# Four filler matmuls taken out of the head stage of an mLSTM block, and one group of transposes issued one step earlier

## What is computed

```
q, k, v, o_pre = projections of rmsnorm(x);  i_pre, f_pre = soft-capped gates
Dmat = Fcum[..., :, None] - Fcum[..., None, :] + i_pre[..., None, :]      # causal
Smat = exp(Dmat - max(Dmat));  C = (q @ k.T) / sqrt(16) * Smat
n    = max(|sum(C)|, exp(-m));  h = (C / n) @ v
h_out = sigmoid(o_pre) * headwise_rmsnorm(h)
x1   = x + h_out @ w_out
out  = x1 + (silu(rms(x1) @ w_gate) * (rms(x1) @ w_up)) @ w_down
```

## Time and profile before

| | |
|---|---|
| runs | 676.15, 677.41, 678.01 us |
| profiled execution | 676.15 us, of which the span of its instructions 674.2 us |
| PE busy | 658.9 us (98%), 5294 matmuls |
| VectorE, ScalarE, GpSimd busy | 438.5, 410.5, 239.2 us |
| mean granted TensorE clock | 0.993 of full |
| head stage (first scores to last back) | 505.0 to 543.6 us |
| FFN of block 3 on TensorE | from 543.6 us |

### The profile page before, as it was taken

One profiled execution on the slowest core, in us unless ns is written; L12 is line 12 of the kernel. 1 busy time (PEld: TensorE's weight loads), 2 busy tenths in 40 slices (PEclk: granted clock), 3 DMA queues, 4 the chain that ended last, 5 costly groups with the idle time before them and its releaser, 6 DMA issues. The chain is left out here.

```text
span 674.2 us, 15272 instructions
## 1 busy us (share of the span) xinstructions
PE 658.9 (98%) x5294; PEld 633.9 (94%) x5294; DVE 438.5 (65%) x970; ACT 410.5 (61%) x1085; POOL 239.2 (35%) x273
## 2 busy tenths in 40 slices
PE   8999999999999999999999989999999999999995
PEld 8999999999999999999999989999987799999995
DVE  6556557556665765765575567556568986556876
ACT  5556677566776666766676863433688964333552
POOL 2731972034353123632338545112450450222101
PEclk9999999999999999999999999999998999999998
DMA  7174664436634446543364304100166100000000
GB/s 253 36 220 155 195 171 139 135 101 174 170 125 111 121 128 180 160 139 106 96 194 130 82 2 151 31 0 7 49 214 221 71 1 1 2 1 0 1 33 31
DMA packets 38156, 69.74 MB, mean 103 GB/s; under 512 B 3424, under 2 KB 22624, under 8 KB 37856
## 3 DMA queue, kind: packets, MB, share of 16 engines
q1 hardware_dynamic: 37680, 68.38, 33.6%
q10 hardware_dynamic: 432, 0.79, 0.4%
HBM read 52.18 MB, written 16.97 MB: 103 GB/s over the span
## 5 line engine op out<-in xcount | busy, mean ns | idle before, releaser
L312 PE MATMUL PJ<-xTh,WBh 128*128 128x256 f32 x364 | 106.7, 293 | 0.0
L314 PE MATMUL PJ<-xTh,WBl 128*128 128x256 f32 x364 | 103.0, 283 | 0.0
L313 PE MATMUL PJ<-xTl,WBh 128*128 128x256 f32 x364 | 102.8, 283 | 0.0
L822 POOL TENSOR_TENSOR stage<-stage 128x256 f32<-128x256 f32 x32 | 24.4, 764 | 164.8 <-DVE stage L689 164.8
L582 ACT ACTIVATE probs<-probs,rinv 128x256 f32<-128x256 f32 x128 | 58.4, 507 | 26.7 <-DVE rinv L705 26.7
L1200 PE MATMUL UG<-xTh,WBh 128*128 (+1 forms) x256 | 73.6, 287 | 1.0 <-PEq L54 1.0
L1203 PE MATMUL UG<-xTh,WBl 128*128 (+1 forms) x256 | 72.4, 283 | 0.0
L1201 PE MATMUL UG<-xTl,WBh 128*128 (+1 forms) x256 | 72.4, 283 | 0.0
L1272 ACT ACTIVATE ga<-UG 128x256 f32<-128x256 f32 x64 | 24.5, 382 | 75.7 <-PE UG L1203 75.7
L312 PEld LDWEIGHTS PJ<-xTh,WBh 128*128 128x128 f32 x364 | 69.6, 191 | 0.6 <-issue 0.2
L313 PEld LDWEIGHTS PJ<-xTl,WBh 128*128 128x128 f32 x364 | 69.6, 191 | 0.0
(11 more groups left out here) (313 smaller groups left out, 2380.5 us busy)
## 6 DMA issues: line engine op xcount, KB each, us to landing
K<-scr_k SPq DMA_DIRECT2D x60, 256.0 KB, 4.5
raw<-in_w_att SPq DMA_DIRECT2D x37, 256.0 KB, 4.7
Q<-scr_q SPq DMA_DIRECT2D x15, 512.0 KB, 7.5
stage<-scr_m SPq DMA_DIRECT2D x6, 768.0 KB, 4.9
scr_q<-rot_h SPq DMA_DIRECT2D x30, 128.0 KB
scr_q<-rot_l SPq DMA_DIRECT2D x30, 128.0 KB
scr_k<-rot_h SPq DMA_DIRECT2D x30, 128.0 KB
scr_k<-rot_l SPq DMA_DIRECT2D x30, 128.0 KB
```

The source lines that it names most:

```text
L312: pe.matmul(out, ah, bh, start=(i == 0), stop=False)
L313: pe.matmul(out, ah, bl, start=False, stop=False)
L314: last = pe.matmul(out, al, bh, start=False, stop=(i == n - 1))
```

## The change

`keep_busy` and its call are removed, and `heads_T(2)` is called after step ht = 0 of the first chunk, behind `back(3, 3)`, rather than after step ht = 1. Everything else is the same, on all engines.

```diff
-            def keep_busy(n):
-
-                for _ in range(n):
-                    pe.matmul(TB[:, :], WLh[:, 0, 0:P], WLh[:, 1, :], start=True, stop=True)
-
...
                     if pair == 2 and c >= 2:
                         project_out(c - 2)
-                    if (c, pair) == (0, 0):
-                        keep_busy(4)
                     values(c, pair)
...
                 if ht == 0:
                     back(3, PAIRS - 1)
+                    heads_T(2)
                 if ht == 1:
-                    heads_T(2)
                     pe_T(pe, 2, 1)
```

## The result

The changed kernel takes 687.43 us (median of four, 685.67 to 689.93), the kernel before beside it 676.78 us (674.55 to 678.01). The ratio is 1.0157 with a 95% interval from 1.0127 to 1.0187: slower, where the forecast was 676.7 us. Ratios in this text leave out executions far above the others of their kernel, among them 15 of the 56 of the kernel before that ran beside the experiments, all above 685 us and with a mean granted clock (0.969 to 0.975) as low as that of the changed kernel (0.965 to 0.977).

What follows compares the result with a forecast made beforehand. The head stage was taken as bound by a VectorE, TensorE and ScalarE loop, the FFN by TensorE. Removing the filler (-1.45 us) and moving heads_T(2) (+0.7) summed to -0.75 us: 676.7 us, range 674.8 to 679.3.

Steps and rivals of the forecast that it cites:

- I now follow TensorE with the same clock, low from 507.72 to 511.13: Head stage, filler removed: the low clock stretch stays where it was, 3.4 us long.
- Rival D: Head stage: without filler the clock returns only with the first project_out; +4.45 us, 681.9 us; chance 0.10.
- the clock holds through all later pairs: Head stage: argument against the clock staying low without the filler, a case given chance 0.10.
- 0.65 us a pair: Head stage: extra cost of a pair at low clock, TensorE's 2.8 us against VectorE's 2.14.
- the whole idle time of 1.45 us goes: Head stage, filler removed: VectorE weighs head 4 at 510.07, not 511.52, a gain of 1.45 us.
- If the low stretch did not exist at all, the filler would cost little: Head stage: at full clock the filler takes 0.9 us and scores still come by 509.8, before VectorE's 510.07.
- Edit 2: FFN start: heads_T(2) one step earlier makes TensorE wait for `ho`; net cost 0.7 us, bounds 0 and 1.0.
- Net cost 0.7 us: FFN start, heads_T(2) moved: a 0.9 us stall less the 0.18 us wait before project_out(2).
- Rival C: FFN start: heads_T(2) finds `ho` ready and gives 0.18; sum -1.6 us, 675.8 us; chance 0.10.
- B: Head stage: TensorE at 1.2 GHz bounds the loop, or the low stretch doubles; +0.55, 678.0 us; chance 0.25.
- the thin place fails: Head stage: values(0, 1), `back` and next scores miss VectorE's 512.21; only 0.0 to 0.2 us of cover; chance 0.25.
- Theory L: Follow-up theory: the clock returns in some executions, not others, with or without filler; two groups about 9 us apart.

Runs made afterwards that it cites:

- e1: Kernel before with only the filler removed, heads_T(2) left in place: 685.75 us, ratio 1.0141.
- e3: Kernel before with the filler's four matmuls reading 32 of the 128 partitions of their operands: 685.4 us, ratio 1.0132.
- e6: Kernel before with two dense matmuls instead of four in the filler before values(0, 0): 684.63 us, ratio 1.0122.
- e2: Kernel before with only heads_T(2) moved one step earlier, filler kept: 675.41 us, ratio 0.9992.
- e4: Kernel before with the filler of four moved from before values(0, 0) to before values(1, 0): 683.57 us, ratio 1.0093.
- e8: Kernel before with six real projection matmuls moved behind scores(0, 1), their copies moved too, filler of four kept: 676.37 us, ratio 0.9975.
- e5: Kernel before with three dense filler matmuls behind scores(0, 1) and none before values(0, 0): 676.08 us, ratio 1.001.

## Why the prediction was wrong

- "I now follow TensorE with the same clock, low from 507.72 to 511.13": this step failed. The forecast kept the low stretch at 3.4 us with the filler gone, but what ended it was the filler. With none (e1 and the changed kernel), a thin one (e3) or half of it (e6) the low stretch lasts 27 to 34 us in the profiles, and all 25 executions of these four kernels have the low mean clock, against 16 of 56 with four dense matmuls. Rival D named this mechanism and had 0.10; it deserved far more.
- Why I gave it 0.10: "the clock holds through all later pairs", that is, sparse pairs at 1.00 in the earlier trace rows. That these pairs keep a full clock says nothing of whether they win it back. At 1.2 GHz the very same pairs left it low for ten of them, with TensorE marked busy nearly all the time. The one row that bore on recovery was the earlier trace rows, with the filler in its stretch, and I read it as a matter of time.
- D's price: "0.65 us a pair". Measured 3.00 - 2.14 = 0.86 us for a plain pair: at the low clock TensorE spends 1.43 us on the values, 0.51 on `back` and 1.06 on the scores (starts at 512.30, 513.73, 514.24 and 515.30 in the kernel after), where D had 2.8 in all. And its end: in the kernel after the first project_out ran at the low clock itself, and the clock came back at 544.6, behind it. D's head stage was 5.2 - 1.45 = +3.75 us; measured is +9.35. From the weighing of head 4 on, the first seven distances between weighings grow by (533.93 - 512.32) - (526.39 - 511.52) = 6.74 us, and the next three, where heads_T(0) and project_out(0) run at the low clock too, by (545.50 - 533.93) - (533.79 - 526.39) = 4.17 us. Those three are the larger omission: D counted no work of the projection and the transposes at half speed.
- "the whole idle time of 1.45 us goes": right. 5.80 - 4.27 = 1.53 us were gained up to the weighing of head 4, and the low clock cost 10.9 us from there to norm_b(2).
- "If the low stretch did not exist at all, the filler would cost little": right, as e2 shows (the weighing of head 4 has no idle time before it). TensorE spent 1.12 us on the filler there, where 0.9 was worked out. In the head part e2 is 38.98 - 37.47 = 1.51 us shorter than the kernel before: the 1.45 us were the price of the low stretch with the filler in it.
- Edit 2, "Net cost 0.7 us": right in place and about right in size, 0.72 us in the kernel after and 0.69 in e2 against the kernel before, 0.4 against e1, with the stall of 0.77 to 0.97 us where it was put and the wait before project_out(2) gone. Rival C is false.
- B, "the thin place fails": not separable, since D came in every execution.
- The rule of the Trainium skill ("TensorE: Matmul & The Clock Gate", Part 1: the throttled clock is the default, activity releases it) was cited against the change, and the outcome went its way. The trace adds that being marked busy isn't enough: in the kernel after TensorE is busy 10.00 of 10 us at 0.50.
- Theory L, that the state of the clock is luck, is half true: the kernel before has long stretches too, in 16 of 56 executions. The filler sets how often: 4 of 4 with two dense matmuls, 16 of 56 with four, 0 of 9 with six (two and six ran on different chips, each beside the kernel before); the changed kernel was long in all 13 executions on record. That the long executions of the kernel before have the same low stretch is read from their mean clock, since none of them was profiled.

What stays open: what exactly makes the clock fall in a given execution, and why the same dense work brings it back in one and not in another. It fell in the head stage of the profiled kernel before, not in that of e2 with the same work up to there, and late in e4 and e8. It is also open whether the rows or the time of the filler count.

## What to carry to other kernels

Work on TensorE that nobody reads may be what holds or restores its clock, so price its removal at both clock levels for the whole sparse stage behind it, and ask of a low stretch in the trace what ended it. That a stage keeps the full clock doesn't show that it could win it back. Dense filler in TensorE's own idle time ahead of a sparse stage cost nothing here and, with the filler of four behind it, went with no long execution in 22. Judge by all executions and their spread, since a median or a ratio can hide the kernel's own long tail.

## What the runs showed of the hardware

Two levels with memory: the same pairs of heads run at 2.4 GHz every 2.14 us, mostly keeping it (but e4 and e8 lost it there), or at 1.2 GHz every 3.00 us, and stay there for 34 us. In two profiles (before, e4) the full clock was back within about 2 us of the end of four dense 128x512 matmuls; twelve dense 128x256 matmuls in e5 were followed by 12.8 us more at the low clock. Matmuls with 32 partitions were issued among others with 32 partitions: four of 512 columns added 0.6 us to TensorE's path, where four with 128 partitions added 1.1. And the "busy" row of TensorE (98% in both kernels) showed nothing of an 11 us loss; the granted clock did.
